# Keys ahead of values, trimmed attention columns, and a new order on every queue, in a windowed cross attention with a top-8 router

## The chip, the core and the metric

One NeuronCore of a Trainium2 chip runs the whole program. The metric is the device time of one execution in microseconds; the median of three runs is compared. TensorE (PE) multiplies, VectorE (DVE), ScalarE (ACT) and GpSimd (POOL) work element by element, and SyncE (SP) issues all DMA transfers. Each engine runs its own list of instructions in order; they meet only through semaphores.

## What is computed

`x` and `ctx` are 16 sequences of 256 channels by 2048 positions in float32. The queries come from the layer norm of `x` over its 2048 positions, keys and values from `ctx`; 8 heads of 32 channels, and each position attends to a window of 16 positions around it. Then a second part takes each of the 256 rows of a sequence as one token of 2048 features: a softmax over 64 experts, of which the 8 largest are kept, scales the row and adds a mixture of expert bias rows.

```python
q = _pointwise(Wq, bq, x)
k = _pointwise(Wk, bk, cond)
v = _pointwise(Wv, bv, cond)
k = jnp.pad(k, ((0, 0), (0, 0), (pad_left, pad_right)))
v = jnp.pad(v, ((0, 0), (0, 0), (pad_left, pad_right)))
...
dots = jnp.einsum('bhdt,bhdtw->bhtw', qh, k_win) * scale
attn = jax.nn.softmax(dots, axis=-1)
out = jnp.einsum('bhtw,bhdtw->bhdt', attn, v_win)
...
scores = jax.nn.softmax(logits, axis=-1)
topk_w, topk_idx = jax.lax.top_k(scores, K_TOP)
w_sum = topk_w.sum(axis=-1, keepdims=True)
...
out = flat * w_sum + bias_mix
...
x = x + jnp.tanh(g_xattn[0]) * _L0_xattn_ref(_layernorm(x, axis=-1), ctx_4096, ...)
x = x + jnp.tanh(g_ffn[0]) * _L0_ffn_ref(_layernorm(x, axis=-1), ...)
```

## The kernel before

**Steps.** `walk` goes over 64 chunks, four of 512 positions for each of the 16 sequences, with a few steps ahead and behind. A step (b, c) mixes stages of several chunks on each engine: projections of keys and values two chunks ahead (`values`, `keys`), queries of the next and this chunk, the scores of this chunk in four units, and for the chunk before `attend`, the output projection, the residual, and the transposes for the router. The 256 channels are two groups g of 128 partitions.

**Arithmetic.** All large products are split: a float32 operand becomes a high part and the rest (`c_hi`, `c_lo`; `x_hi`, `x_lo`; `att_hi`, `att_lo`), and `project` sums three products, six matmuls of 512 columns. ACT makes the high part, GpSimd the low one. Probabilities and values are two float16 halves in one 32-bit word (`part`).

**Scores and softmax.** A unit u is one group and one half of the chunk. PE writes 128 x 384 scores (8 blocks of 48 keys) with 32x32 tiles, into `ps_s[u % 2]`. DVE takes the maximum and subtracts it (`largest`, `shift`), ACT exponentiates, DVE sums and inverts, GpSimd multiplies (`normalise`), ACT and GpSimd make the two halves (`high`, `low`), and DVE transposes 32x32 blocks into `prob_t` (`turn`). Unit 2 and 3 of a chunk wait on PE for `shift` of units 0 and 1, which frees the bank.

**Values.** DVE transposes the chunk's values into `v_turn` (`values_turn`), and eight DMAs of SP spread them to the diagonal blocks of `v_diag`, four a group. `attend` multiplies each of 17 diagonal blocks with the columns of `prob_t` that belong to it, three products each: 51 matmuls. A block of 32 keys meets 64 query columns (32 at both ends).

**The order** is written by hand: each engine's `step` calls its stages in a fixed sequence, with `need` (wait for a semaphore's count). In SP's step the order is the `v_diag` copies, the read of the next context chunk into `c_in` (L366; one buffer, read by ACT as `c_hi` and by GpSimd as `c_lo`), the chunk for the square sums `c_sq` (L372), the residual `x_res`, `x_in`, and for two steps of four the store of a finished half. ACT waits at `c_hi` (L607) for that read, and PE's `scores(1)` waits for `q_col` (L578) of `queries(1)`. DVE's `v_turn` is L853.

**Once a sequence.** DVE makes the layer norm statistics of the next sequence (`ln1`, `inverse_root`); ACT scales the query weights by them and DVE makes their low half `wq_lo`. In the steps of chunk 1 DVE makes the router's logits and weights with tiles `wd` and `lg` in SBUF, and in those of chunks 2 and 3 PE adds four mixtures each (`mixture`), which DVE joins to the rows (`finish`). The values' weights are scaled by a bound from the square sums of the context, so the values of a sequence wait for them; the keys' weights are not.

## Time and profile before

| what | value |
|---|---|
| median of three runs | 1564.99 us (1562.66 to 1567.73) |
| profiled execution | 1567.15 us, its span 1565.0 us |
| TensorE busy | 1469.5 us, 94% |
| VectorE, ScalarE, GpSimd busy | 1269.8, 1148.2, 1148.8 us |
| mean granted TensorE clock | 0.981 of full |
| DMA | 210.39 MB, 134 GB/s |
| `v_diag` copies | 512, 68 KB each |

The page counts an engine as busy while an instruction of it runs; a matmul's end is modelled. The span is the time from the first to the last instruction, the execution's time a little more. A timeline row is one group of equal instructions on an engine: its start in us from the start of the span, how long it took, its line, what it writes and reads, and in brackets how long the engine had been idle before it and what ended that. SPq is the SP queue: there the time is that of issuing, not of the transfer.

### The profile page before, as it was taken

Reading aid. Unit: us, or ns where it says so; the run is one execution under the profiler, and the core shown is the slowest. Engines: PE = TensorE matmul, PEld = TensorE weight load, DVE = VectorE, ACT = ScalarE, POOL = GpSimd, SP = SyncE. Lnnn points to the kernel's source line nnn. Section 1 sums busy time; section 2 is a strip of 40 time slices with the busy share of each in tenths; the row PEclk is TensorE's granted clock in tenths of the full one; section 3 lists DMA queues with packets and bytes.
Section 4 is the critical chain, followed back from the end, with each engine's and each line's share of the span. In section 5 each row is a group of like instructions: output and inputs, shape, how many; then the busy total and the mean of one; then the engine's idle time right before and its main releaser. Section 6 shows DMA issues by size and latency. Waiting matters only on the chain.

```text
span 1565.0 us, 66658 instructions
## 1 busy us (share of the span) xinstructions
PE 1469.5 (94%) x28162; PEld 1210.0 (77%) x28162; DVE 1269.8 (81%) x2970; ACT 1148.2 (73%) x2009; POOL 1148.8 (73%) x1110
## 2 busy tenths in 40 slices
PE   2599999999999999999999999999999999999985
PEld 1477887888888888888888887888888788778764
DVE  4377887889888888988888898888889888888864
ACT  3488777778777877877777787777778787767752
POOL 2487877777787878778787777878777787867762
PEclk8799999999999999999999999999999999999997
DMA  6354455554555455455545545554554555434232
GB/s 202 97 143 125 133 138 133 156 150 102 176 139 136 135 157 142 109 177 139 129 139 157 141 111 179 137 131 137 154 146 110 169 144 132 124 85 132 64 73 93
DMA packets 365577, 210.39 MB, mean 134 GB/s; under 512 B 294497, under 2 KB 295521, under 8 KB 361057
## 3 DMA queue, kind: packets, MB, share of 16 engines
q1 hardware_dynamic: 365280, 206.14, 48.6%
q8 instruction: 223, 3.65, 1.0%
q14 instruction: 74, 0.60, 0.1%
HBM read 136.88 MB, written 33.55 MB: 109 GB/s over the span
## 4 chain that ended last, share of the span: by engine, by line
PE 60%; DVE 26%; issue 7%; POOL 2%; ACT 2%; DMA 1%; SPq 1%; POOLq 0%; DVEq 0%; ACTq 0%
PE ps_j L1099 22%; PE ps_a L1123 9%; PE ps_s L1158 9%; PE ps_s L1099 6%; PE ps_r L1200 6%; DVE prob_t L882 3%; DVE wq_lo L805 2%; PE ps_s L1153 2%; DVE p_sum L872 2%; PE ps_t L1140 2%; PE ps_a L1177 2%; DVE lg L1028 2%; DVE neg_max L861 1%; DVE st_x L889 1%; DVE v_turn L853 1%
## 5 line engine op out<-in xcount | busy, mean ns | idle before, releaser
L474 POOL TENSOR_TENSOR score<-score,p_inv 128x384 f32<-128x384 f32 x256 | 221.8, 867 | 117.2 <-DVE p_inv L876 116.1
L481 POOL TENSOR_TENSOR prob<-score,prob 128x384 f16<-128x384 f32 x256 | 266.1, 1040 | 30.8 <-ACT prob L633 30.0
L1158 PEld LDWEIGHTS ps_s<-kv_win,q_col 32*32 32x32 f32 x16384 | 192.9, 105 | 55.2 <-issue 55.2
L1123 PEld LDWEIGHTS ps_a<-prob_t,v_diag 128*128 128x128 f16 x6528 | 198.9, 97 | 42.3 <-DVE prob_t L882 26.2
L1123 PE MATMUL ps_a<-prob_t,v_diag 128*128 128x64 f16 (+1 forms) x6528 | 212.4, 190 | 19.4 <-DVE prob_t L882 16.0
L1158 PE MATMUL ps_s<-kv_win,q_col 32*32 32x48 f32 x16384 | 228.2, 203 | 1.9 <-issue 1.9
L455 POOL TENSOR_TENSOR c_lo<-c_in,c_hi 128x1024 fp32r<-128x1024 f32 x64 | 152.5, 2382 | 98.6 <-ACT c_hi L607 98.6
L882 DVE STREAM_TRANSPOSE prob_t<-prob 128x512 f32<-128x512 f32 x256 | 176.7, 699 | 54.9 <-POOL prob L481 54.9
L1099 PE MATMUL ps_j<-c_hi,wkv_hi 128*128 128x512 f32 x512 | 170.9, 415 | 39.9 <-POOL c_lo L455 29.9
L450 POOL TENSOR_TENSOR att_lo<-att,att_hi 128x512 fp32r<-128x512 f32 x128 | 162.7, 1275 | 60.2 <-ACT att_hi L593 59.4
L571 ACT ACTIVATE kv_win<-ps_j,v_bias 128x512 f16<-128x512 f32 x128 | 106.5, 844 | 109.7 <-PE ps_j L1099 109.7
L872 DVE TENSOR_REDUCE p_sum<-score 128x8 f32<-128x384 f32 x256 | 139.1, 543 | 57.1 <-ACT score L627 54.0
L633 ACT ACTIVATE prob<-score 128x384 f16<-128x384 f32 x256 | 162.6, 635 | 24.9 <-POOL score L474 24.9
L861 DVE TENSOR_REDUCE neg_max<-ps_s 128x8 f32<-128x384 f32 x256 | 139.6, 545 | 49.9 <-PE ps_s L1158 49.0
L461 POOL TENSOR_TENSOR x_lo<-x_in,x_hi 128x1024 fp32r<-128x1024 f32 x64 | 153.9, 2405 | 21.9 <-ACT x_hi L623 21.9
L627 ACT ACTIVATE score<-score 128x384 f32<-128x384 f32 x256 | 130.4, 515 | 50.6 <-DVE score L867 50.5
L469 POOL TENSOR_TENSOR x<-x,x_res 128x512 f32<-128x512 f32 x128 | 163.0, 1294 | 2.7 <-ACT x L652 2.6
L1099 PE MATMUL ps_j<-c_hi,wkv_lo 128*128 128x512 f32 x512 | 160.8, 396 | 0.0
L1099 PE MATMUL ps_j<-c_lo,wkv_hi 128*128 128x512 f32 x512 | 159.6, 393 | 0.0
L867 DVE TENSOR_TENSOR score<-ps_s,neg_max 128x384 f32<-128x384 f32 x256 | 140.3, 548 | 3.9
L846 DVE SCALAR_TENSOR_TENSOR kv_win<-ps_j,v_bias,kv_win 128x512 f16<-128x512 f32 x128 | 98.6, 793 | 54.0 <-ACT kv_win L571 54.0
L563 ACT ACTIVATE kv_win<-ps_j,bkv_col 128x512 f32<-128x512 f32 x128 | 88.2, 689 | 69.4 <-PE ps_j L1099 62.9
(149 smaller groups left out, 3320.6 us busy)
## 6 DMA issues: line engine op xcount, KB each, us to landing
v_diag<-v_turn SPq DMA_DIRECT2D x512, 68.0 KB, 2.8
c_in<-ctx_dram SPq DMA_DIRECT2D x64, 512.0 KB, 4.8
x_in<-x_dram SPq DMA_DIRECT2D x64, 512.0 KB, 5.6
x_res<-x_dram SPq DMA_DIRECT2D x64, 512.0 KB, 4.4
out_dram<-x SPq DMA_DIRECT2D x32, 1024.0 KB, 7.0
c_sq<-ctx_dram SPq DMA_DIRECT2D x60, 512.0 KB, 5.5
x<-ctx_dram SPq DMA_DIRECT2D x4, 512.0 KB, 6.5
x<-experts_dram SPq DMA_DIRECT2D x2, 512.0 KB, 10.9
```

The lines of the kernel that those rows point to most:

```text
L450: pool.tensor_tensor(att_lo[:, g], att[:, g], att_hi[:, g], ALU.subtract).then_inc(al_rdy[g], 1)
L461: pool.tensor_tensor(x_lo[:], x_in[:, :, cols(ch)], x_hi[:], ALU.subtract).then_inc(xl_rdy, 1)
L469: pool.tensor_tensor(rows, rows, x_res[:, g], ALU.add).then_inc(x1_rdy[g], 1)
L474: pool.tensor_tensor(score[:, u], score[:, u], p_inv[:, u, :].unsqueeze(2).to_broadcast([P, HALF, KEYS]), ALU.mult).then_inc(pm_rdy, 1)
L481: pool.tensor_tensor(part(prob[:, u % 2], 1)[:, :, 0:KEYS], score[:, u], part(prob[:, u % 2], 0)[:, :, 0:KEYS], ALU.subtract).then_inc(pl_ ...
L633: act.activation(part(prob[:, u % 2], 0)[:, :, 0:KEYS], score[:, u], ACT.Copy).then_inc(ph_rdy, 1)
L861: dve.tensor_reduce(neg_max[:, u], scores_of(u), AX, ALU.max, negate=True).then_inc(mx_rdy, 1)
L872: dve.tensor_reduce(p_sum[:, u], score[:, u], AX, ALU.add).then_inc(su_rdy, 1)
L882: dve.transpose(prob_t[:, u // 2, (u % 2) * CHUNK:(u % 2 + 1) * CHUNK], prob[:, u % 2].rearrange("p n k -> p (n k)")).then_inc(pt_rdy, 1)
L1099: ins = pe.matmul(dst[:], w[:, i, o], v[:, i], start=(n == 0), stop=(n == 2 * G + 1))
L1123: ins = pe.matmul(ps_a[g][:, q0:q1], part(v_diag[:, g, j], kv), part(prob_t[:, g, lo:hi], kp), start=(j == 0 and n == 0), stop=(j == NB), ...
L1158: ins = pe.matmul(s[head(h), n * KEYS:(n + 1) * KEYS], q_col[head(h), g, at:at + SUB], kv_win[c % 2][head(h), 0, g, at:at + KEYS], start=F ...
```

## The change

**Columns.** `attend` leaves out the first 16 of the 64 query columns of each block after the first, 48 columns in place of 64, and 16 in place of 32 in the last block. Windows of 16 reach 8 back and 7 on, so these products are zero.

**Keys ahead of values.** `keys` of two chunks ahead come before `values`; `values(1)` comes last in PE's step, and its evacuation by ACT and DVE (`values_high(1)`, `values_low`) moves into the next step. The halo copies of the window edges, one stage for keys and values before, are two; the one-column operation `pool_pad` is gone.

**Order.** All five lists but SP's have a new sequence. In SP's list only the opening changes, and `c_sq` is read one chunk less ahead.

**Router.** `wd` and `lg` lie in the PSUM bank `ps_r`; the column `E` of `wd` is its own tile. The router's first matmuls of a sequence wait for `wd_rdy` in place of `lg_rdy`. The sum of the router weights over features is one reduce on DVE and one matmul in place of 16 matmul instructions.

**Query weights.** ACT writes the scaled weights to `wq_ln` (the space of the raw key weights), rounds them to `wq_hi`, and GpSimd makes `wq_lo`, before by DVE.

**Opening.** Key weights and the first context chunk are read first; `x` ahead of the other weights; GpSimd makes the constants after its first `c_lo`; PE starts with the keys of chunk 0. The split of the expert rows moves from GpSimd to ACT and DVE in later steps. Semaphores of the softmax stages are one a unit.

```diff
-                        lo = max(0, (2 * j - 1) * SUB)
+                        skip = SUB // 2 if j else 0
+                        lo = max(0, (2 * j - 1) * SUB) + skip
                         hi = min(2 * NB * SUB, (2 * j + 1) * SUB)
-                        q0 = max(0, (j - 1) * SUB)
+                        q0 = max(0, (j - 1) * SUB) + skip
                         q1 = min(CHUNK, (j + 1) * SUB)
...
-            for i, w in enumerate((wkT, wvT)):
-                sp.dma_start(wkv_raw[:, i], w.rearrange("(g p) o -> p g o", g=G)).then_inc(kv_ld, 16)
+            sp.dma_start(wkv_raw[:, 0], wkT.rearrange("(g p) o -> p g o", g=G)).then_inc(wk_ld, 16)
+            sp.dma_start(c_in[:], ctx[0, :, cols(0)].rearrange("(g p) t -> p g t", g=G)).then_inc(ctx_in, 16)
+            sp.dma_start(wkv_raw[:, 1], wvT.rearrange("(g p) o -> p g o", g=G)).then_inc(wv_ld, 16)
...
+                def queries_weight_low():
+
+                    need(pool, wqh_rdy, b + 2)
+                    pool.tensor_tensor(wq_lo[:], wq_ln, wq_hi[:], ALU.subtract).then_inc(wql_rdy, 1)
...
+        wd = ps_r[:, LOGITS:LOGITS + G * E].rearrange("p (g e) -> p g e", g=G)
+        lg = ps_r[:, G * E:2 * G * E].rearrange("p (g e) -> p g e", g=G)
...
+                    if live(b, c, -2):
+                        turned_high(0, -2)
+                    if live(b, c, -1):
+                        high(2, -1)
+                    if live(b, c, 2):
+                        context_high(2)
...
+                if live(b, c, 0):
+                    shift(3, 0)
+                    values_turn(0, 0)
...
+                if b == -1 and c == 2:
+                    pe.wait_ge(consts, 1)
+                    pe.wait_ge(wkl_rdy, 1)
+                    keys(0, 2)
+                    keys(1, 2)
+                    pe.wait_ge(wsq_rdy, 2)
```

The order at three places, with what each instruction waits for. First DVE, the head of a step of a chunk 0 before; `score` is the shift of a unit, `neg_max` its maximum, `p_sum` the sum of its exponentials:

```order
L861 TENSOR_REDUCE neg_max<-ps_s 128x8 [waits s_mm]
L853 STREAM_TRANSPOSE v_turn<-kv_win 128x544 [waits vd_ld0,halo_r]
L853 STREAM_TRANSPOSE v_turn<-kv_win 128x544 [waits vd_ld1,halo_r]
L867 TENSOR_TENSOR score<-ps_s,neg_max 128x384 [waits pl_rdy,mx_rdy]
L872 TENSOR_REDUCE p_sum<-score 128x8 [waits e_rdy]
L861 TENSOR_REDUCE neg_max<-ps_s 128x8 [waits s_mm]
L876 RECIPROCAL p_inv<-p_sum 128x8 [waits su_rdy]
L867 TENSOR_TENSOR score<-ps_s,neg_max 128x384 [waits pl_rdy,mx_rdy]
L861 TENSOR_REDUCE neg_max<-ps_s 128x8 [waits s_mm]
L867 TENSOR_TENSOR score<-ps_s,neg_max 128x384 [waits pl_rdy,mx_rdy]
```

And DVE after, the same step, from the maximum of unit 2 to the first statistics:

```order
L888 TENSOR_REDUCE neg_max<-ps_s 128x8 [waits s_mm2]
L873 STREAM_TRANSPOSE v_turn<-kv_win 128x544 [waits vd_ld1,vr_rdy]
L894 TENSOR_TENSOR score<-ps_s,neg_max 128x384 [waits pl_rdy2,mx_rdy2]
L899 TENSOR_REDUCE p_sum<-score 128x8 [waits e_rdy1]
L888 TENSOR_REDUCE neg_max<-ps_s 128x8 [waits s_mm3]
L903 RECIPROCAL p_inv<-p_sum 128x8 [waits su_rdy1]
L894 TENSOR_TENSOR score<-ps_s,neg_max 128x384 [waits pl_rdy3,mx_rdy3]
L873 STREAM_TRANSPOSE v_turn<-kv_win 128x544 [waits vd_ld0,vr_rdy]
L916 BN_STATS st_x<-x_1 128x6 [waits x1_rdy0]
```

Both `v_turn` stood behind the maximum of unit 0; now the one for g = 1 stands behind the maximum of unit 2, and the one for g = 0 behind the shift of unit 3.

Then ACT at the turn from one step to the next, before, in a step of a chunk 1; `x_t` are the turned rows for the router, `q_col` the queries of g = 1:

```order
L599 ACTIVATE x_t<-ps_t 128x512 [waits r_mm,t_mm0]
L641 ACTIVATE c_sq,sq<-c_sq 128x1024 [waits sq_mm,sq_ld]
L607 ACTIVATE c_hi<-c_in 128x1024 [waits k_mm1,cl_rdy,k_mm0,ctx_in]
L578 ACTIVATE q_col<-ps_s,bq_col 128x512 [waits s_mm,q_mm1]
L599 ACTIVATE x_t<-ps_t 128x512 [waits r_mm,t_mm1]
L585 ACTIVATE att<-ps_a,v_unscale 128x512 [waits al_rdy0,av_mm0]
L593 ACTIVATE att_hi<-att 128x512 [waits o_mm1,o_mm0,ae_rdy0]
```

And after, in a step of a chunk 0:

```order
L606 ACTIVATE x_t<-ps_t 128x512 [waits r_mm,t_mm0]
L642 ACTIVATE prob<-score 128x8x48 [waits pt_rdy0,pm_rdy2]
L615 ACTIVATE c_hi<-c_in 128x1024 [waits k_mm1,v_mm1,v_mm0,cl_rdy,k_mm0,ctx_in]
L606 ACTIVATE x_t<-ps_t 128x512 [waits r_mm,t_mm1]
L592 ACTIVATE att<-ps_a,v_unscale 128x512 [waits al_rdy0,av_mm0]
L576 ACTIVATE kv_win<-ps_j,v_bias 128x512 [waits vleft_rdy,vt_rdy1,v_mm1]
L583 ACTIVATE q_col<-ps_s,bq_col 128x512 [waits s_mm3,q_mm1]
L600 ACTIVATE att_hi<-att 128x512 [waits o_mm1,o_mm0,ae_rdy0]
```

The context square has left the head of the step; `c_hi` has come to the third place, and between it and `q_col` there are now the turned rows, the attention copy of g = 0 and the values' high part of g = 1.

Last PE, the waits of the first half of a step of a chunk 3, before (rows that wait for nothing are left out; the first `ps_s` row with `xl_rdy` is `queries(1)`, those with `ident_b` open a score unit):

```order
L1123 MATMUL ps_a<-prob_t,v_diag 128x32 [waits ae_rdy0,fin_rdy,vd_ld0,pt_rdy]
...
L1099 MATMUL ps_s<-x_hi,wq_hi 128x512 [waits sh_rdy,xl_rdy]
...
L1140 MATMUL ps_t<-ident,x_0 128x128 [waits xt_rdy0,x1_rdy1]
...
L1153 MATMUL ps_s<-mask,ident_b 128x384 [waits halo_r,qh_rdy0]
...
L1123 MATMUL ps_a<-prob_t,v_diag 128x32 [waits ae_rdy1,fin_rdy,vd_ld1,pt_rdy]
...
L1200 MATMUL ps_r<-wr,x_t 128x64 [waits xt_rdy1]
...
L1153 MATMUL ps_s<-mask,ident_b 128x384 [waits qh_rdy1]
...
L1153 MATMUL ps_s<-mask,ident_b 128x384 [waits sh_rdy]
```

And after, a little further:

```order
L1142 MATMUL ps_a<-prob_t,v_diag 128x32 [waits ae_rdy0,vd_ld0,fin_rdy,pt_rdy1,pt_rdy0]
...
L1159 MATMUL ps_t<-ident,x_0 128x128 [waits xth_rdy0,x1_rdy1]
...
L1172 MATMUL ps_s<-mask,ident_b 128x384 [waits kr_rdy,qh_rdy0]
...
L1116 MATMUL ps_s<-x_hi,wq_hi 128x512 [waits sh_rdy3,xl_rdy]
...
L1142 MATMUL ps_a<-prob_t,v_diag 128x32 [waits ae_rdy1,vd_ld1,fin_rdy,pt_rdy3,pt_rdy2]
...
L1172 MATMUL ps_s<-mask,ident_b 128x384 [waits qh_rdy1]
...
L1220 MATMUL ps_r<-wr,x_t 128x64 [waits xth_rdy1]
...
L1172 MATMUL ps_s<-mask,ident_b 128x384 [waits sh_rdy0]
...
L1197 MATMUL ps_a<-ex_hi,wd_both 128x512 [waits ae_rdy0,wt_rdy]
...
L1116 MATMUL ps_j<-att_hi,wo_hi 128x512 [waits vl_rdy0,al_rdy1,al_rdy0]
...
L1197 MATMUL ps_a<-ex_hi,wd_both 128x512 [waits ae_rdy1,wt_rdy]
...
L1172 MATMUL ps_s<-mask,ident_b 128x384 [waits sh_rdy1]
```

`queries(1)` now comes after the first score unit, and one of the two output projections after the last. The unit that waits for `qh_rdy1` comes right behind the second attend, and in this step two mixtures stand ahead of the unit that waits for `sh_rdy1`.

## Rows read from the trace of the kernel before

**Rows 1.** The page, part 1: TensorE busy, share of the span, weight loads, other engines.

```profile
PE 1469.5 (94%) x28162; PEld 1210.0 (77%) x28162; DVE 1269.8 (81%) x2970; ACT 1148.2 (73%) x2009; POOL 1148.8 (73%) x1110
```

**Rows 2.** Stretches of four steps: length, busy of each engine, clock, DMA share, GB/s.

```profile
811.30:833.60 22.30, 21.89 (x437) 17.98 (x436) 20.93 (x66) 18.28 (x37) 16.77 (x18) 1.00 0.48 121
833.60:857.20 23.60, 23.60 (x447) 19.65 (x446) 20.38 (x43) 17.96 (x32) 18.83 (x18) 1.00 0.42 106
857.20:881.50 24.30, 23.66 (x443) 19.36 (x443) 21.74 (x49) 17.82 (x31) 16.86 (x18) 1.00 0.54 151
881.50:902.80 21.30, 21.30 (x435) 17.73 (x434) 15.74 (x30) 17.12 (x29) 18.56 (x19) 1.00 0.66 192
```

**Rows 3.** Timeline of PE in the opening: start, us, line, operation, wait before it.

```profile
52.48 1.22 PE L1099 MATMUL ps_j<-c_hi,wkv_hi 128*128 128x512 f32 x2 [24.31 <-POOL c_lo L455]
```

**Rows 4.** Timeline of PE in the step of a chunk 0.

```profile
881.50 1.64 PE L1123 MATMUL ps_a<-prob_t,v_diag 128*128 128x32 f16 x51
882.99 0.71 PE L1099 MATMUL ps_s<-x_hi,wq_hi 128*128 128x512 f32 x2
...
887.46 1.98 PE L1200 MATMUL ps_r<-wr,x_t 128*128 128x64 f32 x16
889.27 0.33 PE L1153 MATMUL ps_s<-mask,ident_b 128*128 128x384 bf16 x1
...
891.42 0.74 PE L1099 MATMUL ps_j<-att_hi,wo_hi 128*128 128x512 f32 x2
...
894.33 0.34 PE L1153 MATMUL ps_s<-mask,ident_b 128*128 128x384 bf16 x1
```

**Rows 5.** Timeline of ACT: start of that step, and two later operations of another.

```profile
884.29 1.05 ACT L607 ACTIVATE c_hi<-c_in 128x1024 fp32r<-128x1024 f32 x1
885.24 0.68 ACT L578 ACTIVATE q_col<-ps_s,bq_col 128x512 f32<-128x512 f32 x1
885.81 0.59 ACT L599 ACTIVATE x_t<-ps_t 128x512 f32<-128x512 f32 x1
...
852.38 0.86 ACT L571 ACTIVATE kv_win<-ps_j,v_bias 128x512 f16<-128x512 f32 x1 [0.51 <-PE ps_j L1099]
```

**Rows 6.** Timeline of DVE in the step of a chunk 2.

```profile
839.59 1.36 DVE L853 STREAM_TRANSPOSE v_turn<-kv_win 128x544 f32<-128x544 f32 x2
...
845.91 0.55 DVE L861 TENSOR_REDUCE neg_max<-ps_s 128x8 f32<-128x384 f32 x1
846.50 0.56 DVE L867 TENSOR_TENSOR score<-ps_s,neg_max 128x384 f32<-128x384 f32 x1
```

**Rows 7.** Timeline of the SP queue in the step of rows 4.

```profile
887.35 6.33 SPq L359 DMA_DIRECT2D v_diag<-v_turn  x8
893.72 0.62 SPq L366 DMA_DIRECT2D c_in<-ctx_dram  x1
```

**Rows 8.** The tile c_in, read by SP: from issue to landing, 64 reads.

```profile
DMA to landing us min/median/max: 3.9/4.8/6.9
```

**Rows 9.** PE at three waits over 1.9 us, and the clock after the first.

```profile
1367.84 1.70 PE L1123 MATMUL ps_a<-prob_t,v_diag 128*128 128x32 f16 x51 [2.40 <-DVE prob_t L882]
...
1394.53 1.64 PE L1123 MATMUL ps_a<-prob_t,v_diag 128*128 128x32 f16 x51 [1.98 <-DVE prob_t L882]
...
1465.99 1.64 PE L1123 MATMUL ps_a<-prob_t,v_diag 128*128 128x32 f16 x51 [2.40 <-DVE prob_t L882]
...
1369.25:1376.00 6.75, 6.75 (x116) 0.50 0.48 72
```

**Rows 10.** Groups of DVE: the router's logits, whole run.

```profile
L1028 DVE SCALAR_TENSOR_TENSOR lg<-wd,rs_x,rb 128x64 f32<-128x64 f32 x32 | 28.6, 933 | 0.0
...
L1023 DVE SCALAR_TENSOR_TENSOR wd<-wr_sum,neg_mean_x,ps_r 128x64 f32<-128x64 f32 x32 | 7.5, 274 | 0.1
```

**Rows 11.** Timelines of SP and of GpSimd in the opening.

```profile
15.04 8.36 SPq L346 DMA_DIRECT2D x<-experts_dram  x2
...
16.93 2.34 POOL L455 TENSOR_TENSOR c_lo<-c_in,c_hi 128x1024 fp32r<-128x1024 f32 x1 [5.91 <-ACT c_hi L607]
```

More of the change, by code:

```diff
@@ L211, in gated_window_attention_and_router @@
         av_mm = pair("av_mm")
[L212 removed]
+        s_mm = unit("s_mm")
         o_mm = pair("o_mm")
@@ L1278, in step, with keys @@
-                if before:
-                    rows(0, -1)
-                if live(b, c, 2):
-                    keys(0)
-                    keys(1)
-                if b == -1 and c == 3:
-                    pe.wait_ge(r_ld, 16 * 4)
-                    for k in range(T // P):
-                        ins = pe.matmul(ps_r[:, 0:E], all_ones[:], wr[:, k], start=(k == 0), stop=(k == T // P - 1))
-                    ins.then_inc(sum_mm, 1)
+                def keys(g, off):
+                    need(pe, cl_rdy, nth(b, c, off))
+                    if live(b, c, off - 3):
+                        need(pe, ob_rdy[g], nth(b, c, off - 3))
+                    else:
+                        need(pe, vl_rdy[g], nth(b, c, off - 1))
+                    project(ps_j[g], wkv_hi[:, 0], wkv_lo[:, 0], g, c_hi, c_lo).then_inc(k_mm[g], 1)
@@ L1290, in _ @@
+                if b == 0 and c == 0:
+                    pe.wait_ge(wrp_rdy, 1)
+                    pe.matmul(ps_r[:, WRSUM], all_ones[:], wr_part[:], start=True, stop=True).then_inc(sum_mm, 1)
             walk(step)
```

1124 lines of the change are left out of this document (571 added, 553 removed).

## The prediction

> **What bounds the kernel now.** The page comes first: TensorE is busy for 94% of the span [rows 1], and its longest wait, 24.31 us, is in the opening [rows 3]. The table of stretches, cut at the four chunk steps of one sequence, says it more sharply: the steps of chunks 1, 2, 3 and 0 last 22.3, 23.6, 24.3 and 21.3 us, 91.5 together, and PE is busy in all but 1.05 us of them, while DVE is busy for 15.7 to 21.7, ACT for about 18, GpSimd for 17 to 19 [rows 2]. So the kernel before is its matmul stream, and a change is worth what it takes from that stream, unless it makes the stream wait. Whether it does is read from the timelines of PE, ACT, DVE and the SP queue, held against the new order.
>
> **The trimmed columns.** One attend is 51 matmuls in 1.49 us (881.50 to 882.99), 29.2 ns each [rows 4]. 45 of the 51 go from 64 columns to 48. If the pace follows the columns, an attend loses 45 x 7.3 ns = 0.33 us; if the weight load of each matmul sets the pace, nothing. I take 0.2, between the two: 128 attends, 0 to 42 us, taken as 26, 0.4 a step. The Trainium skill (TensorE: Matmul & The Clock Gate, section "Wait — 56ns, not 53.3ns?") says that the start-to-start time of matmuls does not drop below about 25 ns, however few their columns. By it the attend would save 45 x 4.2 ns = 0.19 us, an estimate from that page; no row here prices 48 columns in this shape.
>
> **The new order, and the read it delays.** This is the term that decides. Four queues form a ring that is closed once in each step:
> - SP issues the eight `v_diag` copies, and behind them the read of the next context chunk into `c_in`, the only buffer. The copies wait for `v_turn`; SP's order is unchanged.
> - Before, `values_turn` for g = 0 stood right behind the first maximum; the copies began 5.9 us into the step (887.35 against 881.50) and `c_in` was issued at 893.72 [rows 4, 7]. With a landing of 4.8 us [rows 8] it was there at 898.5, and its reader `c_hi` ran at about 2.8 us into a step (884.29) [rows 5]: over 5 us of slack.
> - Now `values_turn(0)` stands behind `shift(3)`, which needs PE's last score unit. And `c_hi` moves from behind the context square to the third place in ACT's step, ahead of the attention copy, `values_high(1)` and `queries_high(1)`, for which `scores(1)` on PE waits.
>
> The ring, from the landing of `c_in`:
> - ACT: `c_hi` 0.95 start to start, the turned rows and the attention copy 0.57 each (as `q_col` has it), `kv_win` 0.86, `q_col` 0.68 [rows 5]: 3.63.
> - PE: `scores(1)` and `scores(2)` 2.15 together, the router 1.81, `output(0)` 1.46 (half of 891.42 to 894.33), `scores(3)` 1.08 [rows 4]: 6.50.
> - DVE: maximum to shift 0.59, shift 0.56, turn 0.68 [rows 6]: 1.83.
> - SP: first copy to the issue of `c_in` 6.37 [rows 7]; landing 4.8 [rows 8]: 11.17.
>
> Sum 23.1, plus a hand-over or so: 23.2 us for chunk 0. PE's own work in that step is 21.3 - 0.4 = 20.9. The ring is longer by 2.3, so PE waits that long ahead of `scores(1)` (in chunk 2 partly ahead of the turned weights). For chunk 1, DVE has the logits, the maxima and the replacements ahead of its last maximum, seven small operations of 0.15 to 0.3 us (the first kind has 0.275) [rows 10], of which some 1.1 don't fit into its wait: 24.3. For chunks 2 and 3 two of the four mixtures stand ahead of `scores(3)`, 2 x 0.57 (a quarter of 23.6 - 21.3) [rows 2], and one `finish`, about the size of a shift, ahead of `shift(3)`: 24.8 each. Together 97.1 against 91.5, or 5.6 more a sequence; over 15 sequences +84. Queued behind the waiting `c_hi` are the whole rest of ACT's step, and behind that PE, DVE and GpSimd: nothing covers it. The 26 us of the trim are already in it; they don't reach the end, since they lie in the part of PE's step that waits.
>
> **The clock.** Three waits of PE at one place were 2.40, 1.98 and 2.40 us long; 1.4 us after the first one ended, the granted clock was 0.50 (1.2 GHz) for 6.75 us, and after the two others it stayed at 1.00 [rows 9]. A fall costs half of 6.75, 3.4 us, and it comes just behind the wait, in the PE part of the ring, so the ring is longer by it. The changed kernel has about 60 waits of 2.2 to 3.3 us (24.3 - 21.0 in the longest). One in three falls by the rows, and I take somewhat more for the longer ones: two in five, 24 x 3.4 = +82. Bounds: none (0) and each (+204).
>
> **The router's tiles in PSUM.** `lg<-wd` with all operands in SBUF takes 1080 ns for 64 columns, and `wd<-ps_r`, as large and with one input in PSUM, takes 275 [rows 10]. The Trainium skill (SBUF — State Buffer, section "Who interferes with whom") says that a DVE instruction with two SBUF inputs and a GpSimd instruction that reads SBUF exclude each other for the whole instruction. The trace agrees, 1080 against 275 ns. Worth up to 2 us of DVE a sequence, and DVE is not what is waited for: 0. If the ring didn't bind, it would shorten the small waits of chunks 1 and 3.
>
> **Edits with one answer.** Query weight halves: two DVE operations leave, one of GpSimd and one of ACT come, once a sequence and outside the ring: 0. Halos apart and the lost pad: 0.1 us of GpSimd, which has 2 us to spare a step. Keys ahead of values: the same matmuls; `kv_win`'s value half comes later, which is why `values_turn` moved. More semaphores: 0.
>
> **The opening.** Before, `c_lo` of the first chunk began at 16.93 [rows 11], and the second chunk's projection started at 52.48 [rows 3]. Keys need no scale: issued at about 1, landed 4.8 later, `c_hi` 1.05 and `c_lo` 2.34 [rows 5, 8, 11] let them start at about 9.2. The second chunk's read is behind the experts' load, which holds SP from 15.04 to 23.4 [rows 11]; with the same three terms its projection starts at about 32, 20 us earlier. The 32 matmuls of the router's weight sum (two routers' 16, 2 x 1.81) [rows 4] shrink to one, but other first work, the statistics of `x` above all, then becomes the limit. I take -19 in all (-10 to -25).
>
> **The end.** The last three steps read no context: -2 for the trim. The kernel before also lost some 7 us in the fall of [rows 9] and the wait beside it; -7.
>
> Sum: 1565.0 (the span) + 84 + 82 - 19 - 2 - 7 = 1703. The profiled execution took 2.2 us more than its span, and the median of the runs is 2.2 below it, so the sum stands against the median as it is: about **1700 us**, 9% slower.
>
> **Rivals.**
> - *The ring binds, the clock holds.* For it: two of the three waits. Time: 1700 - 82, about 1619, still slower.
> - *Each wait drops the clock.* 1619 + 204 = 1823. Against it: the same two waits.
> - *The read is hidden (faster).* The ring stops binding if the copies and the landing together take 8.9 us instead of 11.2, or if ACT doesn't reach `c_hi` as early as its list says. For it: the shortest landing is 3.9 [rows 8], and idle queues may serve the copies faster. Against it: even with 3.9 the copies would have to be through in 5.0 us, against 6.37 [rows 7]. Then PE bounds: per sequence -1.6 for the trim and -1.05 for waits, 15 x 2.65 = 40, with opening and end 1565 - 40 - 28 = 1497. With the ring short by 1 us only and no falls, 1619 - 60 = 1559: the point from which the sign turns is a pair of 10.3 us.
> - *The change does less than it says* (the trim saves nothing): no effect while the ring binds, +26 in the rival before.
>
> **Chances and range.** Ring with some falls, about 1640 to 1770: 0.54. Ring without falls, 1600 to 1640: 0.2. Falls nearly everywhere, over 1770: 0.1. Hidden: faster 0.14, and 0.02 within 0.3%, which is about what a measurement of this kernel can tell from no change. The range 1600 to 1800 leaves out 0.16 below and about 0.04 above.
>
> **What would show it.** Right: waits of over 2 us on PE at `scores(1)` behind `q_col`; ACT idle ahead of `c_hi` with the `c_in` read as its releaser, in nearly all steps; `c_in` issued 6 to 7 us behind a late `v_turn`; a sequence of 97 to 106 us; PE under 90% busy, and clock tenths under 9 in many slices. The attend is about 1.3 us. Wrong: `c_hi` not waiting for its read, a sequence of 88 us. A sequence near 97 with the clock at 1.00 throughout would show the ring right and the clock term wrong.

## The result and the profile after

The changed kernel takes 2020.4 us (median of 4 runs, 2002.4 to 2033.7), the kernel before 1566.4: a ratio of 1.286 (95% interval 1.281 to 1.291), which leaves out the slowest of the four as a slow run. The prediction was 1700 us in a range of 1600 to 1800. The direction was right; the loss is 454 us instead of 134.

The page of the changed kernel (parts 1 and 2: busy time and share; the clock that was granted in tenths; part 4: shares of the chain that ended last):

```profile
PE 1604.2 (80%) x28132; PEld 1305.1 (65%) x28132; DVE 1224.2 (61%) x2957; ACT 1148.0 (57%) x2027; POOL 1154.4 (57%) x1188
...
PEclk7887878979879988798778978889988989978897
...
PE 33%; DMA 24%; SPq 22%; DVE 12%; issue 8%; ACT 1%; POOL 0%; DVEq 0%; POOLq 0%; ACTq 0%
```

PE is busy for 80% where it was for 94% [rows 1], and for 1604 us although its stream got shorter: it ran at half clock for part of the time. Of the chain that ended last, 46% is DMA and SP's queue. The same table of stretches as in [rows 2], for four steps of one sequence (length, busy of PE, PEld, DVE, ACT, POOL, granted clock, DMA share, GB/s):

```profile
1180.50:1213.50 33.00, 26.93 (x437) 21.95 (x436) 20.60 (x61) 18.05 (x37) 17.60 (x19) 0.79 0.30 81
1213.50:1244.20 30.70, 25.00 (x447) 20.33 (x446) 20.27 (x37) 18.58 (x33) 18.25 (x19) 0.89 0.33 88
1244.20:1275.10 30.90, 24.26 (x443) 19.80 (x442) 18.73 (x48) 18.20 (x32) 18.60 (x20) 0.89 0.44 126
1275.10:1308.80 33.70, 26.66 (x435) 21.73 (x434) 16.82 (x40) 16.43 (x28) 17.12 (x19) 0.75 0.39 110
```

128.3 us a sequence, against 91.5 before and 97.1 (without clock falls) in the prediction. What is waited for (the list of waits: total, times, longest):

```profile
DVE st_in L798 <- DMA x_in<-x_dram: 430.6, 59, 10.1
...
PE ps_a L1142 <- DVE prob_t L909: 341.6, 61, 7.9
...
ACT c_hi L615 <- DMA c_in<-ctx_dram: 211.7, 63, 8.8
```

The third line is the wait that the prediction named. The first is one that it did not: `next_stats(1)`, the statistics of `x` (`st_in`), is the first operation of DVE's step, ahead of the turns of `prob` for which attend(1) waits, and it waits for the read of `x_in`. One round of that ring in the timelines, DVE, SP, DVE and PE in this order:

```profile
1222.37 0.69 DVE L798 BATCH_NORM_STATS2 st_in<-x_in 128x6 f32<-128x512 f32 x1 [6.86 <-DMA x_in<-x_dram]
...
1237.34 0.72 DVE L873 STREAM_TRANSPOSE v_turn<-kv_win 128x544 f32<-128x544 f32 x1
...
1238.10 5.32 SPq L373 DMA_DIRECT2D v_diag<-v_turn  x8
1243.46 0.62 SPq L380 DMA_DIRECT2D c_in<-ctx_dram  x1
1244.13 0.48 SPq L386 DMA_DIRECT2D c_sq<-ctx_dram  x1
1244.71 0.41 SPq L392 DMA_DIRECT2D x_res<-x_dram  x1
1245.16 0.47 SPq L398 DMA_DIRECT2D x_in<-x_dram  x1
...
1253.39 0.69 DVE L798 BATCH_NORM_STATS2 st_in<-x_in 128x6 f32<-128x512 f32 x1 [8.23 <-DMA x_in<-x_dram]
1254.00 1.29 DVE L909 STREAM_TRANSPOSE prob_t<-prob 128x512 f32<-128x512 f32 x2
...
1255.35 2.13 PE L1142 MATMUL ps_a<-prob_t,v_diag 128*128 128x32 f16 x51 [6.64 <-DVE prob_t L909]
```

From st_in to st_in: 15.0 us of DVE and PE work up to `v_turn(0)`, 0.8 to the first copy, 5.4 for the eight copies, 1.7 for three other reads ahead of `x_in`, and 8.2 until it has landed: 31.0. Followed back from its end over the whole run, the last chain goes through the read of `x_in` in 59 steps and through that of `c_in` in 3. The landing alone was 5.6 us in the kernel before; here (issues, KB each, median us to landing) it is longer. The four reads are issued within 2.2 us, as all that SP waited for between them is done by then; in the kernel before, `x_res` waited for the residual, and 3.6 us passed from the end of `c_sq`'s issue to that of `x_res` (825.83 to 829.47):

```profile
c_in<-ctx_dram SPq DMA_DIRECT2D x64, 512.0 KB, 4.9
x_in<-x_dram SPq DMA_DIRECT2D x64, 512.0 KB, 8.1
```

### The profile page after: what moved, and what is told of

The parts are those of the page before. It is cut to its first block, busy times and chain, and to the rows that moved or that the text cites. A ratio compares the mean times of both kernels' runs of the same rounds, so it can differ in the third digit from the quotient of the medians.

```text
span 2014.3 us, 66851 instructions
## 1 busy us (share of the span) xinstructions
PE 1604.2 (80%) x28132; PEld 1305.1 (65%) x28132; DVE 1224.2 (61%) x2957; ACT 1148.0 (57%) x2027; POOL 1154.4 (57%) x1188
## 4 chain that ended last, share of the span: by engine, by line
PE 33%; DMA 24%; SPq 22%; DVE 12%; issue 8%; ACT 1%; POOL 0%; DVEq 0%; POOLq 0%; ACTq 0%
DMA x_in<-x_dram 23%; SPq L373 16%; PE ps_s L1177 9%; PE ps_r L1220 8%; PE ps_a L1142 7%; PE ps_j L1116 5%; DVE prob_t L909 4%; DVE v_turn L873 3%; PE ps_s L1172 2%; SPq L380 2%; SPq L386 2%; DVE score L894 1%; SPq L392 1%; DVE wkv_lo L845 1%; PE ps_a L1197 1%
## 5 line engine op out<-in xcount | busy, mean ns | idle before, releaser
L1142 PE MATMUL ps_a<-prob_t,v_diag 128*128 128x48 f16 (+2 forms) x6528 | 226.2, 196 | 342.1 <-DVE prob_t L909 341.6
L1142 PEld LDWEIGHTS ps_a<-prob_t,v_diag 128*128 128x128 f16 x6528 | 214.7, 106 | 384.0 <-DVE prob_t L909 365.8
L798 DVE BATCH_NORM_STATS2 st_in<-x_in 128x6 f32<-128x512 f32 x128 | 86.9, 683 | 430.6 <-DMA x_in<-x_dram 430.6
L1177 PEld LDWEIGHTS ps_s<-kv_win,q_col 32*32 32x32 f32 x16384 | 232.8, 121 | 67.5 <-issue 67.5
L1177 PE MATMUL ps_s<-kv_win,q_col 32*32 32x48 f32 x16384 | 270.9, 223 | 0.5 <-issue 0.4
L592 ACT ACTIVATE att<-ps_a,v_unscale 128x512 f32<-128x512 f32 x128 | 87.5, 683 | 299.0 <-PE ps_a L1142 298.9
L661 ACT ACTIVATE x<-ps_j,bo_col 128x512 f32<-128x512 f32 x128 | 88.0, 687 | 194.7 <-PE ps_j L1116 194.5
L615 ACT ACTIVATE c_hi<-c_in 128x1024 fp32r<-128x1024 f32 x64 | 67.8, 1059 | 211.9 <-DMA c_in<-ctx_dram 211.7
L1220 PE MATMUL ps_r<-wr,x_t 128*128 128x64 f32 x1024 | 162.6, 325 | 0.7 <-ACT x_t L606 0.7
L1220 PEld LDWEIGHTS ps_r<-wr,x_t 128*128 128x128 f32 x1024 | 152.9, 236 | 7.1 <-ACT x_t L606 0.9
```

Of the source, the lines that this page charges most:

```text
L1142: ins = pe.matmul(ps_a[g][:, q0:q1], part(v_diag[:, g, j], kv), part(prob_t[:, g, lo:hi], kp), start=(j == 0 and n == 0), stop=(j == NB), ...
L1177: ins = pe.matmul(s[head(h), n * KEYS:(n + 1) * KEYS], q_col[head(h), g, at:at + SUB], kv_win[(c + off) % 2][head(h), 0, g, at:at + KEYS], ...
L1220: ins = pe.matmul(wd[:, g], x1_t[:, g, k], wr[:, ch * TB + k], start=(ch == 0 and k == 0 and g == 0), stop=(ch == NCH - 1 and k == TB - 1) ...
```

## The experiments

Theory A, after the trace: the loss is this ring (late `v_turn(0)`, eight copies, reads behind them, st_in at DVE's head), with the predicted one through `c_in` as a second and shorter one, and the clock on top. Rivals: the new order on PE and ACT is itself the cause (B), the transfers are slow by themselves (C), only `c_in`'s ring binds (A2), the clock is most of it.

**Which read binds (e1, e2, e3).** SP's step in the changed kernel is: copies, `c_in`, `c_sq`, `x_res`, `x_in`, `out`.

```
e1: + c_in, c_sq, x_in ahead of the copies     - the same behind them
e2: + c_in, c_sq ahead of the copies           - the same behind them
e3: + x_in ahead of the copies                 - the same behind them
```

> The changed kernel, with three reads of SP's step (`c_in`, `c_sq`, `x_in`) put ahead of the eight `v_diag` copies; `x_res` and `out` stay behind. Nothing else. Theory A (the delay is the two reads queued behind a late `v_turn`, plus the clock falls that the waits bring): both rings open, PE waits no longer than 0.5 us ahead of attend(1) or scores(1), the clock stays at 1.00, and the time is that of the rival 'the read is hidden', about 1500 us (1480 to 1540), faster than the kernel before. Theory B (the new order on PE, ACT and DVE is itself the cause, the queue only shows it): the waits move to other tiles and the time stays over 1800. Theory C (the transfers themselves are slow, x_in landing 8 us after its issue): the time stays over 1700, since the same bytes move.

> The changed kernel, with only `c_in` and `c_sq` put ahead of the eight `v_diag` copies; `x_in` stays last of the four reads. Theory A1 (the ring through x_in is the longer one and binds): it is only shorter by the two issues that left from ahead of x_in, about 2 x 0.6 = 1.2 us a step, so about 2020 - 60 x 1.2 = 1950 us (1880 to 1980), DVE still waits at st_in for the x_in read. Theory A2 (my prediction's ring, through c_in, is the one that binds, and x_in's lateness only follows it): near 1500 us.

> The changed kernel, with only `x_in` put ahead of the eight `v_diag` copies; `c_in` is read behind them as before. Theory A1 (x_in's ring binds in the changed kernel, c_in's is a second, shorter one): the x_in wait at DVE's st_in goes, and what is left is the ring that the prediction worked out, 24.3 us a step and a fall of the clock of 3.4 us in some or all steps, so 1620 (no falls) to 1820 us (a fall in each step). Theory A2 (c_in's ring is the one): unchanged, about 2020 us, or longer by the issue of x_in. Theory D (both rings are opened by this alone, as the copies' wait is not the late part): 1500 us.

Measured: e1 1687.7 us (ratio to before 1.078, 1.074 to 1.082), e2 1795.4 (1.146, 1.141 to 1.150), e3 1743.5 (1.110, 1.104 to 1.116). A2 falls with e2 and e3: with `c_in` early, DVE still waits for `x_in`, and with `x_in` early that wait is gone and the time falls by 277 us. Since nothing but SP's order was touched and up to 333 us went, B and C can't be the main cause. They aren't excluded as a part: e1 still stands 121 us above the kernel before, and only 12 under C's bound of 1700. Two sizes were missed. e2 came out 155 us below what was expected: besides 1.2 us of issues, the landing of `x_in` fell from 8.1 to 5.5 us, as two reads fewer were ahead of it. And e1 was to be near 1500 and is 190 above; more on that below. e3 is the kernel that the prediction described, with no wait for `x_in`. Its four steps and three of its waits, from an execution of 1756.4 us:

```profile
899.10:921.80 22.70, 21.53 (x438) 17.56 (x437) 20.70 (x59) 17.98 (x37) 17.61 (x19) 1.00 0.41 116
921.80:950.30 28.50, 25.40 (x448) 20.61 (x448) 20.03 (x39) 18.38 (x33) 18.07 (x19) 0.94 0.40 100
950.30:975.80 25.50, 23.25 (x444) 18.89 (x443) 22.38 (x48) 18.31 (x32) 18.65 (x20) 1.00 0.50 148
975.80:1005.60 29.80, 25.34 (x436) 20.58 (x436) 17.11 (x40) 16.53 (x29) 17.21 (x19) 0.83 0.45 125
...
ACT c_hi L615 <- DMA c_in<-ctx_dram: 206.5, 64, 7.8
...
PE ps_a L1142 <- issue: 41.3, 28, 2.2
PE ps_s L1172 <- ACT q_col L583: 31.9, 23, 2.4
```

All 64 `c_hi` wait for their read, and the sequence is 106.5 us. That is not simply the prediction's 97.1 with falls of the clock added. The steps last 22.7 to 29.8 us, where 23.2 to 24.8 were worked out; the last chain goes through the read of `c_in` in 34 of 64 steps, not in all; and PE waits at `scores(1)` for `q_col` only 23 times, 31.9 us in all, while it stands for 41.3 us ahead of attend with no releaser that the profile knows ("issue", more on it below).

**The head of the ring (e5, e8).** e5 moves it forward in the changed kernel, e8 puts it into the kernel before, and does nothing else.

```
e5, DVE of the changed kernel:            e8, DVE of the kernel before:
      invert(0, 0)                              largest(0)
+     values_turn(0, 0)                   -     values_turn(0)
+     values_turn(1, 0)                         values_turn(1)
...                                       ...
-     values_turn(1, 0)
...
      shift(3, 0)                               shift(3)
-     values_turn(0, 0)                   +     values_turn(0)
```

> The changed kernel, with both `values_turn` put behind invert(0) on DVE, ahead of the second maximum of the step (the earliest place at which the value halo is there without a wait); SP's order is that of the changed kernel. Theory A (both rings begin at the late v_turn(0)): in the trace of the changed kernel v_turn(0) began at 1237.34 and invert(0) ended at 1230.0, so the copies, and the four reads behind them, start about 6 to 7 us earlier; the ring of 30.6 us falls to about 24, and what clock falls are left come with it: 1600 to 1680 us. With PE as the bound it would be 1500. Theory B (the late turn doesn't matter, as the reads are slow by themselves or the new PE order is the cause): over 1950 us.

> The kernel before, with only values_turn(0) moved behind shift(3) on DVE, as the changed kernel has it. Theory A (the late head of the ring is enough, since in this order too DVE's statistics of x stand at the head of its step and SP reads behind the copies): the copies start at about 14 instead of 6 us into a step, x_in lands about 5 us after it is wanted, 27 to 29 us a step with falls of the clock: 1750 to 1900 us. Theory B (the new PE, ACT and DVE order is needed for the loss): 1560 to 1600 us, as the slack of over 5 us ahead of c_hi takes it up.

Measured: e5 1656.2 us (1.058, 1.054 to 1.062), e8 2016.7 (1.289, 1.286 to 1.292). e8 is the plainest result of the study: one transpose of 0.73 us, moved down one list in the kernel before, makes it as slow as the whole change does. Neither the new PE order nor the new ACT order is needed. Its ring has the same head, the late turn with the copies and reads behind it, but it closes at another reader (chain by line; two groups with their idle time; DVE's wait; the late turn and the copies):

```profile
DMA c_sq<-ctx_dram 16%; SPq L359 15%; PE ps_s L1158 9%; PE ps_r L1200 9%; PE ps_j L1099 7%; DMA x_in<-x_dram 3%; DVE v_turn L853 3%; ACT c_hi L607 2%; PE ps_s L1153 2%; SPq L366 2%; DVE neg_max L861 2%; DVE wq_lo L805 2%; ACT q_col L578 1%; PE ps_a L1177 1%; DVE p_sum L872 1%
...
L1200 PE MATMUL ps_r<-wr,x_t 128*128 128x64 f32 x1024 | 213.6, 396 | 130.5 <-ACT x_t L599 130.4
...
L641 ACT ACTIVATE c_sq<-c_sq 128x1024 f32<-128x1024 f32 x59 | 62.3, 1056 | 315.5 <-DMA c_sq<-ctx_dram 315.5
...
DVE st_in L787 <- DMA x_in<-x_dram: 402.2, 59, 9.5
...
1211.20 0.73 DVE L853 STREAM_TRANSPOSE v_turn<-kv_win 128x544 f32<-128x544 f32 x1
...
1211.96 5.32 SPq L359 DMA_DIRECT2D v_diag<-v_turn  x8
```

ACT's old order has the context square ahead of `c_hi`, `q_col` and the turned rows `x_t` for which PE waits, and the square waits for `c_sq`, the second read behind the copies. The last chain goes through that read in 51 steps and through `x_in` in 8. DVE's statistics wait for `x_in` too, but in its old list the turns of `prob` stand ahead of them. e8 was expected at 1750 to 1900, with `x_in` as the read. So it shows what the late head costs, not through which read; since the two rings close at different readers, it is chance that their times are within 4 us of each other. e5, the same step undone in the changed kernel, takes away 364 of the 454 us.

**The clock (e6).** 24 matmuls go into PE's wait, with a result that is overwritten. The waits for `prob_t` and `v_diag` come behind them, that for the free bank stays ahead (the code is shortened):

```
 def attend(g, off):
+    if g == 1 and live(b, c, 0):
+        for _ in range(24):
+            pe.matmul(ps_a[g][:, 0:HALF * KEYS], ident_b[:], mask, start=True, stop=True)
     for u in (2 * g, 2 * g + 1):
         need(pe, pt_rdy[u], nth(b, c, off))
```

> The changed kernel, with 24 extra matmuls (the mask's own operands, 384 columns, 0.16 to 0.25 us each, so 4 to 6 us) on PE ahead of each attend(1), where PE waits 6 us or so for prob_t behind x_in's read. Their result is overwritten by the attend; the output is the reference's. Only PE's activity in the wait changes. Theory A (the clock falls behind that wait lie in the ring, 3.4 us each in nearly every step): granted clock near 1.00, the step shorter by about 3, so 1810 to 1860 us. Theory E (the ring is all DMA and issue, PE's part of it small): the clock is back but the time stays within 30 us of 2020. Theory F (extra matmuls only lengthen PE's stream): over 2020.

Measured: 1938.6 us (1.240, 1.233 to 1.248), 82 us less than the changed kernel, with a mean granted clock of 0.956 instead of 0.856. PE still waits behind the extra work:

```profile
1225.96 4.07 PE L1132 MATMUL ps_a<-mask,ident_b 128*128 128x384 bf16 x24
...
1232.55 1.43 PE L1146 MATMUL ps_a<-prob_t,v_diag 128*128 128x32 f16 x51 [2.52 <-DVE prob_t L909]
```

So the clock is at least a fifth of the loss, since 0.956 is not 1.00; 160 to 210 us had been expected of it. One reason for less shows in the changed kernel's stretches around the wait that ends at 1255.35:

```profile
1248.20:1251.70 3.50, 0.50 (x3) 0.07 (x1) 0.00 (x0) 3.29 (x6) 2.16 (x1) 0.99 1.03 368
1251.70:1255.30 3.60, 0.00 (x0) 0.00 (x0) 1.91 (x4) 0.60 (x2) 1.45 (x2) 0.50 0.66 277
1255.30:1258.50 3.20, 3.15 (x92) 2.83 (x96) 2.85 (x15) 0.95 (x2) 0.00 (x0) 0.50 0.02 5
1258.50:1262.00 3.50, 3.50 (x122) 3.16 (x111) 3.39 (x9) 3.24 (x7) 2.54 (x3) 1.00 0.00 0
```

The clock is at 0.50 (1.2 GHz) from 1251.7 to 1258.5. In a long wait it falls before the wait is over, and the 3.6 us of it that lie in the wait cost nothing. Only 3.2 us of work ran at half speed: 1.6 us lost. Not every fall is so cheap. Counted over the whole run in stretches of 1 us, the changed kernel has 578 us at half clock in 65 pieces, and PE works in 407 of them; in e6 it is 167 and 141. That is 266 us less of work at half clock, or 133 us of PE's time, of which 82 reached the end.

**The trim (e4, e7, e11, e17).** Undone in two kernels with their reads or turns moved (`skip = 0`), put alone into the kernel before, and put on top of e16 (below).

> The kernel with the three reads ahead of the copies, and the attend's columns back to 64 (the trim undone). Its difference to the kernel with the trim prices the trim where PE is (by theory A) the bound: 0.20 us an attend, as measured between the two traces (1.49 and 1.29), 128 attends, about +26 us. If something else than PE bounds there, the difference is near 0.

> The kernel before, with the trimmed attention columns alone. By theory A, PE bounds there and an attend is 0.20 us shorter: 128 x 0.2 = 26 us, about 1540 us. If the trim frees PE time that turns into waits, and waits let the clock fall (the kernel with the reads first was 24 us slower with the trim than without), it is 1560 to 1600 us.

Measured: e4 1663.9 us (1.063, 1.059 to 1.068), so without the trim the kernel e1 is 24 us faster. The profiled clocks go with it, 0.965 against 0.938: some 90 us less at half clock, or up to 45 us, against 26 us more work (an estimate from these two traces). e7 1562.9 (0.998, 0.996 to 1.000): the trim alone is worth 0 to 6 us in the kernel before, not 26. Its steps beside those of [rows 2]:

```profile
807.80:830.00 22.20, 21.54 (x437) 17.59 (x437) 20.98 (x67) 18.32 (x37) 16.78 (x18) 1.00 0.49 129
830.00:853.40 23.40, 23.27 (x448) 19.26 (x448) 20.33 (x43) 17.98 (x32) 18.85 (x18) 1.00 0.43 102
853.40:877.60 24.20, 23.39 (x443) 19.05 (x442) 21.85 (x49) 17.86 (x31) 16.77 (x17) 1.00 0.53 150
877.60:898.50 20.90, 20.90 (x435) 17.33 (x434) 15.71 (x30) 16.92 (x29) 18.52 (x19) 1.00 0.67 196
```

PE's busy time fell by 1.36 us in these four steps, their length by 0.8: only chunk 0's step gives the whole 0.4 back, the others 0.1 to 0.2 each. There PE waits a little longer instead (its idle time in the four grew from 1.04 to 1.60). The mean clock fell from 0.981 to 0.973, which goes against the rest: the three of e7's ten runs with a clock of 0.978 to 0.980 took 1556.5 to 1559.2 us, and those at 0.971 to 0.973 took 1563.9 to 1568.2. PE's issue waits over 0.5 us (see below) grew too, from 2 with 2.5 us to 10 with 8.4.

**What remains once the ring is open (e9, e10, e11).** e1 and e5 stay 90 to 120 us above the kernel before, with less matmul work and an opening 20 us shorter. e9 opens the ring in e5's way and eases what was left of it (`x_in` second of the reads, the statistics behind the turns of `prob`), e10 also restores PE's old head of the step, and e11 is e10 without the trim.

```
e9 = e5, SP:  - c_in, c_sq, x_res, x_in    + c_in, x_in, x_res, c_sq   (behind the copies)
         DVE: - next_stats(1); turn(3, -1); turn(2, -1)
              + turn(3, -1); turn(2, -1); next_stats(1)
e10 = e9, PE: - rows(1, -2); scores(0, 0); queries(1, 0)
              + queries(1, 0); rows(1, -2); scores(0, 0)
e11 = e10:    + skip = 0
```

> The changed kernel, with three moves: both `values_turn` behind invert(0) (as in e5_turns_early), SP's reads behind the copies in the order `c_in`, `x_in`, `x_res`, `c_sq` (x_in second instead of last), and next_stats(1) on DVE behind the two turns instead of ahead of them. Theory A (in e5 what is left of the ring is x_in's landing of 7.2 us as the last of four reads, and the stats ahead of prob_t's turns): the DMA waits at st_in (72.9 us in e5) fall below 20 and are no longer PE's; about 40 to 60 us faster than e5: 1590 to 1620 us. Theory G (what is left in e5 is PE's instruction issue while the reads run, and the clock): 1640 to 1660, as in e5.

> e9_combo, with PE's step in the old order at its head: attend(0), queries(1), rows(1), scores(0) instead of attend(0), rows(1), scores(0), queries(1). In the new order 102 + 8 + 129 instructions of attend, rows and scores stand together, and in e1 and e5 PE stood in the middle of such runs of scores matmuls with nothing to wait for ('issue', 57.9 and 28.7 us, 2.9 in the kernel before), with the DMA engines at 400 GB/s. Theory G (issue: PE's instructions come through the same DMA engines and can't be brought at that rate while a burst runs): the projection between gives time to fetch, the issue waits fall by half or more, 15 to 40 us faster than e9. Theory H (the issue waits have another source): no change.

> e10_combo_queries with the 64-column attend (the trim undone). By PE's work alone it is 26 us slower. If what the trim frees turns into waits and these let the clock fall (reads first: 24 us faster without the trim; the kernel before: the trim was worth 2 us of 26), it is the same or up to 25 us faster.

Measured: e9 1596.4 us (1.019, 1.016 to 1.022), e10 1628.7 (1.037, 1.033 to 1.042), e11 1622.0 (1.035, 1.032 to 1.038). In e9 the wait of st_in is 5.8 us in all (430.6 in the changed kernel, 72.9 in e5), as expected: the ring is gone. e9 still stands 30 us above the kernel before, although its opening is 20 us shorter, so some 50 us belong to the rest of the new order, and theory B is right to that extent. What PE then waits for without a releaser that the profile knows ("issue"), in e1, e9, e10 and e13 in this order:

```profile
PE ps_s L1177 <- issue: 57.9, 42, 2.6
...
PE ps_s L1176 <- issue: 35.0, 33, 2.1
...
PE ps_s L1176 <- issue: 12.0, 21, 1.0
...
PE ps_s L1187 <- issue: 54.8, 37, 3.0
```

In the kernel before it is 1.9 us on the same tile. In e10 it fell as theory G says, but the time rose by 32 us. scores(0) came later, shift(0) stood behind the chain of ln1 in chunk 3's step, PE waited up to 1.9 us there, and falls of the clock came behind: its mean is 0.948 against 0.971 in e9. e14, below, takes these waits away and wins little, so this account of the 32 us is not the whole. The trim shows no worth there either (the intervals of e10 and e11 overlap).

**The chains, the reads' start (e12 to e15, e18).**

```
e12 = before, SP:       + c_in ahead of the copies
e13 = e9,  DVE, step 3: - ln1; shift(0)                      + shift(0); ln1
           DVE, step 1: - ln2's last two rounds; turn(3), turn(2)
                        + turn(3), turn(2); ln2's last two rounds
e14 = e10, the same;    e15 = e14, SP: + c_in ahead of the copies
e18 = e13, SP:          + c_in ahead of the copies
```

> The kernel before, with only the read of `c_in` moved ahead of the eight copies on SP. There the ring has slack, so no wait goes. Theory G (a read issued some 5 us into a step, while PE goes through the dense runs of scores, holds up PE's instructions): the issue waits rise from 2.9 us to 20 or more and the time to 1580 to 1610 us. Theory H: 1566 us, unchanged.

> e9_combo with two chains of small DVE operations moved: ln1 behind shift(0) instead of ahead of it (chunk 3's step), and the last two of the three rounds of ln2's root behind the two turns at the head of chunk 1's step instead of ahead of them. In e9 PE waited 1.67 us ahead of attend(1) in each step of chunk 1 and 0.9 us for shift(0) in each of chunk 3, behind these chains. Theory I (each wait is paid as such, and nothing falls behind it in e9): 15 x (1.6 + 0.9) = 37 us, about 1560 us. Theory J (DVE is itself near its limit in these steps, so the chain's time is paid elsewhere in the step): under 10 us, about 1590 us.

> e10_combo_queries with the same two moves. In e10 the wait for shift(0) in chunk 3's step was 2.04 us, and a fall of the clock came behind it, together 4 us a sequence. Theory I with the clock (waits of about 2 us bring a fall, and go together with it): 15 x (1.75 + 4) = 86, about 1545 us, faster than the kernel before and than e13, as the issue waits are smaller here. Theory J: 1600 to 1620 us.

> e14_chains_moved_queries with the `c_in` read ahead of the eight copies on SP. The reads behind the copies are then 512 KB fewer and should be through before the next step's dense runs of matmuls. Theory G (issue waits come from reads that still run at the head of the next step): issue waits fall below e14's, 5 to 15 us faster. Against it: in the kernel before the same move cost 12 us. Then 10 to 15 us slower than e14.

> e13_chains_moved with the `c_in` read ahead of the eight copies on SP, nothing else. Theory G (PE's instructions wait behind reads that still run when the next step's attend, rows and scores begin): issue waits fall from 54.8 us to 25 to 40, and the time by as much and the falls behind them, 1565 to 1580 us. Theory H (the issue waits belong to PE's order and not to the reads): 54 us of issue waits again and 1598 us.

Measured: e12 1578.7 us (1.008, 1.003 to 1.013), e13 1597.9 (1.020, 1.016 to 1.025), e14 1620.9 (1.033, 1.029 to 1.037), e15 1600.5 (1.022, 1.017 to 1.027), e18 1593.9 (1.016, 1.013 to 1.019). In e13 the waits behind the chains went (PE's wait for prob_t fell from 29.2 us in e9 to 5.7), and the issue waits grew by 20: a gain at one wait was paid at the next, and theory I's 1560 us did not come. e14 missed by more. Expected at 1545, it took 1620.9, and its interval overlaps that of e10. PE's wait for the shift fell from 29.3 us to 1.7 and that for `prob_t` from 36.1 to 10.6, but the issue waits rose from 12.0 to 39.2 with PE's order unchanged. One of the issue waits, in e13's timeline of PE and in stretches around it (length, busy of the engines, clock, DMA share, GB/s):

```profile
661.62 0.78 PE L1187 MATMUL ps_s<-kv_win,q_col 32*32 32x48 f32 x51
664.82 0.36 PE L1187 MATMUL ps_s<-kv_win,q_col 32*32 32x48 f32 x13 [2.42 <-issue]
...
658.00:662.00 4.00, 4.00 (x100) 3.28 (x102) 3.90 (x13) 3.94 (x7) 4.00 (x8) 1.00 1.03 384
662.00:663.00 1.00, 0.40 (x35) 0.26 (x23) 1.00 (x1) 1.00 (x3) 1.00 (x1) 1.00 0.32 115
663.00:664.00 1.00, 0.00 (x0) 0.00 (x0) 1.00 (x1) 0.47 (x1) 1.00 (x1) 1.00 0.00 0
```

And the DMA queues by kind (packets, MB, share of 16 engines) in three stretches of it, 648.9 to 662.2, 662.2 to 663.4 and 663.4 to 664.9, the last of which is empty, and below them in the whole run:

```profile
q1 hardware_dynamic: 5539, 2.62, 72.0%
...
q1 hardware_dynamic: 29, 0.03, 7.6%
q8 instruction: 1, 0.02, 5.4%
...
q8 instruction: 224, 3.67, 0.9%
```

PE stops in the middle of 64 matmuls whose operands are all there, just after 4 us in which the 16 DMA engines were full (share 1.03). For 13 us no packet of the instruction queue had come; one of 16 KB ran from 662.29 to 663.33, and PE went on 1.49 us after its end. This is the rule and no single case. In the 20 traces together PE has 364 issue waits over 0.5 us, and 354 of them end 1.2 to 1.7 us after the end of such a packet. In e13, 16 of the 34 counts of PE's matmuls and weight loads from one such stop to the next are exact multiples of 256 (56264 of them came in 224 packets, 251 each). So the first half of theory G holds: in its issue waits PE waits for its own instructions, and the DMA engines bring them.

The second half, that data transfers make them late, is not settled. For it: in e13 the data queue's share was over 0.9 in the 3 us ahead of 28 of the 35 late packets, and ahead of 15 of the other 189. Against it: in the kernel before 32 packets came behind such stretches and PE stood at none of them, and in e18 it is 16 of 41. The earlier `c_in` lowered the issue waits in e15 (39.2 to 25.7 us; the time fell by 20 us) and left them in e18 (54.8 to 54.4, where G expected 25 to 40), and in e12 they came to 10.1 us on all tiles, from 6.5 in the kernel before, against G's 20, though e12 is 13 us slower.

**The opening alone (e16, e17).**

```
e16 = before, SP:  - rb, wr, experts, c_sq ahead of the second c_in   + the same behind it
              DVE: + stats of x, ln1 ahead of the first projections
              ACT: + second chunk's c_hi; then gates, query weights, squares
e17 = e16 + the trimmed columns
```

> The kernel before with another opening, its steps unchanged: the reads of the router's weights and of the experts on SP behind the second context chunk's read, the statistics of x on DVE ahead of the first projections, and on ACT the second chunk's c_hi ahead of the query weights and of the two squares. In the trace of before PE waited 24.31 us, until 52.48, for that chunk. Theory K (the opening is a plain latency, and what it saves reaches the end): first attend at 60 to 66 us instead of 81.4, so 1566 - 15 to - 21 = 1545 to 1551 us, faster than both kernels. Theory L (later waits for the weights and the experts take it back): 1560 to 1566 us.

> e16_before_opening with the trimmed columns. By e7 the trim was worth 2 us of the 26 that PE's work becomes shorter: so 0 to 6 us faster than e16. By the work alone 26 us.

Measured: e16 1558.0 us (0.994, 0.991 to 0.996), e17 1555.2 (0.992, 0.990 to 0.993). Both beat both kernels. In e16 PE's waits for the second chunk's `c_lo` and for `x_lo` are 4.14 and 6.88 us, in place of the one of 24.31 [rows 3]. The first attend is at 72.7 instead of 81.4, less than expected, and all of it reaches the end. As with e7 the trim is worth 3 us, within the two intervals.

## Why the prediction was right in direction and wrong in the ring that binds

1. **The head of the ring: right.** "Now `values_turn(0)` stands behind `shift(3)`", so the copies and the reads behind them start late. e5 takes this back and 364 of the 454 us go; e8 makes this move alone in the kernel before and loses as much as the change, there through `c_sq`.
2. **Which read closes the ring: the step that failed.** The prediction followed "the read that it delays" to `c_in` and its reader `c_hi`, and stopped. SP issues `x_in` behind the same copies, three reads later, and its reader stands even earlier in a step than `c_hi`, at the head of DVE's. Through `x_in` the ring is 31.0 us instead of 23.2 to 24.8. The ring through `c_in` is real, but its size was not confirmed. e3, where it is left alone, takes 1743.5 us, inside the range, and that is partly luck: the read binds in 34 of 64 steps. From the first copy to the issue of `c_in` the changed kernel takes 5.36 us and not 6.37; with the landing of 4.9 that is the pair of 10.3 us at which, by the prediction's own rival, the sign would turn. Waits for PE's instructions, for which the sum had nothing, are 63 us in e3 (41.3 and 21.8).
3. **The landing: a term that was not free to be copied.** 4.8 us for `c_in` held (4.9). For `x_in` it went from 5.6 to 8.1 us, as the reads now come in one bunch; no row of before showed that.
4. **The clock: the size came out near by luck.** The term was +82, and e6 gives back 82 with the clock still at 0.956. But the term was 24 falls of 3.4 us behind waits of 2.2 to 3.3 us, and the sum's own rows give waits of 2.8, 1.6, 1.5 and 2.3 us for the four steps (24.3, 24.8, 24.8 and 23.2 less PE's work). The changed kernel has waits of about 7 us and 65 pieces at half clock, about one a step, with a mean length of 8.9 us. In e3, the kernel of the sum, the clock of 0.905 is 333 us at half clock, against 59 in the kernel before: up to 137 us lost.
5. **The trim: right per attend, wrong in worth.** The changed kernel's attend takes 1.29 us (1244.21 to 1245.50), 0.20 less than 1.49 [rows 4], as taken. The 25.3 ns a matmul agree with the floor of about 25 ns that the Trainium skill gives (TensorE: Matmul & The Clock Gate, section "Wait — 56ns, not 53.3ns?"). That it would give 0.4 us a step wherever PE bounds was wrong: 0 to 6 us in all (e7).
6. **"PE bounds the kernel now": too strong.** [rows 2] show PE busy in nearly all of each step, but by e7 three of the four steps give back 0.1 to 0.2 us where PE's work in them shrinks by 0.27 to 0.35. The rival's 1497 us was not reached by any variant: of the changed kernel's variants with the ring open the best took 1594.
7. **The router's tiles: right.** `ps_r<-ps_r,rs_x,rb` now takes 283 ns against 933 in [rows 10] (the prediction's 1080 is that of one step and not the mean that stands there), 21 us of DVE over the run. It was not put back by itself, so that nobody waits for it is read from the lists of waits alone.
8. **The opening: right.** The first attend is at 60.07 instead of 81.40, 21 us earlier (-19 was taken). e16 and e17 show that such a gain, small as it is, is the one part of the change that clearly arrives.

## What to carry to other kernels

When a step is moved later on a queue, list everything that this queue issues behind it, and for each the first reader on every engine; the ring that binds is the one with the longest tail and the earliest reader, not the first one found. With the same late head it was `x_in` on DVE in one order and `c_sq` on ACT in the other. Copy a landing time only if the same transfers run beside it before and after. And a stream that is busy for 98% of a step is not thereby what bounds it: take something away (as in e7) before pricing what shortens it.
